# Softmax denominators of four token tiles in one 128-column block, and a new order of steps on four engines

## The reference

```python
x = x + tanh(g_xattn[0]) * xattn(layernorm(x), ctx, ctx, ...)
x = x + tanh(g_ffn[0]) * ffn(layernorm(x), w_gate, w_expert, b_expert)

# xattn: 16 heads of 32 features
scores = einsum('bhqd,bhkd->bhqk', Q, K) / sqrt(32)
out = einsum('bhqk,bhkd->bhqd', softmax(scores), V)
expert = (einsum('bsd,eod->ebso', out, We) + be).mean(axis=0)
return expert @ Wo.T + bo

# ffn: gate over 8 experts, the first 100 tokens that choose an expert are taken
best = argmax(softmax(hs @ w_gate)); locations = cumsum(one_hot(best)) - 1
combined = combine @ (dispatched @ w_expert + b_expert)
```

## Time and profile before

| | |
|---|---|
| time, median of 3 runs | 405.29 us (405.26 to 406.44) |
| the profiled execution | 405.64 us, span 403.9 us |
| granted TensorE clock | 1.000 in the whole span but its last microseconds |
| PE | busy 396.3 us (98%), 3102 matmuls |
| DVE | busy 333.3 us (83%) |
| ACT | busy 225.3 us (56%) |
| POOL | busy 167.4 us (41%) |

### The profile page before, as it was taken

One profiled execution on the slowest core, in us unless ns is written; L12 is line 12 of the kernel. 1 busy time (PEld: TensorE's weight loads), 2 busy tenths in 40 slices (PEclk: granted clock), 3 DMA queues, 4 the chain that ended last, 5 costly groups with the idle time before them and its releaser, 6 DMA issues.

```text
span 403.9 us, 8706 instructions
## 1 busy us (share of the span) xinstructions
PE 396.3 (98%) x3102; PEld 182.2 (45%) x3102; DVE 333.3 (83%) x662; ACT 225.3 (56%) x320; POOL 167.4 (41%) x157
## 2 busy tenths in 40 slices
PE   7999999999999999999999999999999999899996
PEld 4556454443444444444444434444444444354444
DVE  6548456986898989998998998899897589779996
ACT  4436323568566754947485486748556474775110
POOL 2028999215080247309033530713271064460371
PEclk9999999999999999999999999999999999999999
DMA  8999991466059408823960692295169016241585
GB/s 278 334 389 394 344 390 41 91 124 165 2 111 199 174 1 170 217 98 85 175 223 1 142 238 104 60 183 189 54 133 242 5 33 175 84 132 28 99 172 180
DMA packets 65901, 63.19 MB, mean 156 GB/s; under 512 B 42277, under 2 KB 45617, under 8 KB 65859
## 3 DMA queue, kind: packets, MB, share of 16 engines
q1 hardware_dynamic: 60747, 56.19, 50.9%
q0 software_dynamic: 1632, 3.49, 3.1%
q10 hardware_dynamic: 3480, 2.96, 2.2%
HBM read 29.59 MB, written 12.98 MB: 105 GB/s over the span
## 4 chain that ended last, share of the span: by engine, by line
PE 71%; DVE 2%; issue 1%; ACT 1%; POOL 1%; DVEq 0%; ACTq 0%; POOLq 0%
PE ps L840 71%; ACT probs L1234 1%; PE ps L1161 0%; DVE xb L1567 0%; POOL known L1929 0%; POOL rstd L1929 0%; DVE bn_raw L1573 0%; ACT xn_hi L1234 0%; DVE xn L1500 0%; DVE base_cnt L1653 0%; DVE place_hot L1723 0%; POOL veps L1927 0%; ACT part_x L1234 0%; DVE xb L1865 0%; DVE wqT_lo L1678 0%
## 5 line engine op out<-in xcount | busy, mean ns | idle before, releaser
L1234 ACT ACTIVATE probs<-ps 120x1024 f32<-120x1024 f32 x64 | 62.0, 1024 | 19.4 <-PE ps L840 19.4
L1602 DVE TENSOR_REDUCE neg_max<-ps 128x16 bf16<-128x1920 f32 x32 | 68.7, 2148 | 3.7 <-PE ps L840 3.7
L1989 POOL TENSOR_TENSOR attn_lo<-attn,attn_hi 128x512 f16<-128x512 f32 x28 | 31.8, 1158 | 91.0 <-ACT attn_hi L1234 91.0
L840 PE MATMUL ps<-xnT_hi,wqT_hi 128*128 128x512 f16 x128 | 48.6, 380 | 0.0
L840 PE MATMUL ps<-mixT_hi,attn_hi 128*128 128x512 f16 x128 | 48.5, 379 | 0.0
L840 PE MATMUL ps<-mixT_lo,attn_hi 128*128 128x512 f16 x128 | 48.5, 379 | 0.0
L840 PE MATMUL ps<-xnT_lo,wqT_hi 128*128 128x512 f16 x128 | 48.5, 379 | 0.0
L1997 POOL TENSOR_TENSOR xb<-xb,mix_bias 128x512 f32<-128x512 f32 x32 | 39.6, 1271 | 15.4 <-DVE cb_col L1544 15.4
L1234 ACT ACTIVATE q_hi<-ps,bias_cols 128x512 f16<-128x512 f32 x32 | 22.1, 692 | 31.4 <-PE ps L840 31.4
L840 PE MATMUL ps<-q_stack,k_stack 97*128 97x512 f16 x128 | 33.9, 381 | 1.2 <-ACT probs L1234 1.0
L840 PE MATMUL ps<-probs,den_sel 120*32 120x256 f32 x512 | 34.1, 384 | 0.0
(11 more groups left out here) (279 smaller groups left out, 792.7 us busy)
## 6 DMA issues: line engine op xcount, KB each, us to landing
xb<-in_x_dram SPq DMA_DIRECT2D x8, 1024.0 KB, 6.1
q_stack<-q_hi SPq DMA_DIRECT2D x48, 128.0 KB, 2.4
out_dram<-xb SPq DMA_DIRECT2D x6, 1024.0 KB, 7.4
raw<-in_L_xattn_We_dram SPq DMA_DIRECT2D x5, 1024.0 KB, 10.3
q_stack<-q_lo SPq DMA_DIRECT2D x32, 128.0 KB, 2.4
xb<-in_L_xattn_We_dram SPq DMA_DIRECT2D x3, 1024.0 KB, 10.3
k_stack<-k_scratch SPq DMA_DIRECT2D x8, 360.0 KB, 4.6
k_scratch<-k_hi ACTq DMA_DIRECT2D x16, 120.0 KB, 7.9
```

The lines of the kernel that those rows point to most:

```text
L840: return e.matmul(out_, a, b, start=start, stop=stop, **kw)
L1234: return e.activation(out_, in_, func, **kw)
L1602: e.tensor_reduce(maxed[:, :, :, g], quad[:, :, 0:NT * SK].rearrange("p j (t s) -> p t j s", t=NT), AX.X, ALU.max, negate=True).then_inc(s ...
L1989: e.tensor_tensor(attn_lo[:, g, :], attn[:, g, :], attn_hi[:, g, :], ALU.subtract).then_inc(s_alo, 1)
```

## The change

Three things change.

1. The denominators of all four token tiles stand in 128 columns. `weight_sums` makes four products of 128 columns for each row group where it made two of 256; the selection matrix is one row of `den_sel` of which a window is taken. `reciprocal`, `rden_high` and `rden_low` work on 128 columns where they had 256. `spread_rden` makes four products of 128 columns where it made two of 256. The setup builds `head_sel` with four DVE instructions of 512 columns instead of two.
2. The tables of PE, ACT, DVE and POOL are written in another order.
3. The first of the units that are done beside batch 0's queries (`N_FIRST`) waits for `route_x_out` of batch 0, since `route_x` now stands ahead of it by less.

The core of the diff:

```diff
-        den_sel = sb("den_sel", [SK, 2 * NK * DK + 24], F32)
-        head_sel = sb("head_sel", [P, 2, NK, P], F16)
+        den_sel = sb("den_sel", [SK, 2 * DK + NK], F32)
+        head_sel = sb("head_sel", [P, NT, NK, P], F16)
...
-        rden = sb("rden", [P, SH], F32)
+        rden = sb("rden", [P, SQ], F32)
...
+                if i == N_FIRST:
+                    e.wait_ge(s_pxe, 1)
...
-                for h in range(2):
-                    sel = den_sel[:, (h * NK + g) * DK:(h * NK + g + 1) * DK]
+                for t in range(NT):
+                    first = SEL_AT - (2 * t * NK + g)
                     for j in range(HJ):
                         row = slice(j * DK, (j + 1) * DK)
-                        ins = mm(den_b[row, 0:SH], sel, probs[:, g % 2, j, h * SH:(h + 1) * SH],
-                                 start=(g == 0 and h == 0), stop=(g == NK - 1 and h == 1))
+                        ins = mm(den_b[row, 0:SQ], den_sel[:, first:first + DK], probs[:, g % 2, j, t * SQ:(t + 1) * SQ],
+                                 start=(g == 0 and t == 0), stop=(g == NK - 1 and t == NT - 1))
...
-                mm(bank[:, 0:SH], head_sel[:, 0, g, :], rden_both[:, :])
-                mm(bank[:, SH:S], head_sel[:, 1, g, :], rden_both[:, :]).then_inc(s_bc, 1)
+                for t in range(NT):
+                    ins = mm(bank[:, t * SQ:(t + 1) * SQ], head_sel[:, t, g, :], rden_both[:, :])
+                ins.then_inc(s_bc, 1)
...
             run(range(0, B - 2), [
-                (logits, -1, 0), (table_rows, -2, 0), (scores, 0, 1), (values, 0, 0), (scores, 0, 2),
+                (logits, -1, 0), (table_rows, -2, 0), (scores, 0, 1), (values, 0, 0), (values, 0, 1),
+                (route_x, 1, 0), (scores, 0, 2), (q_begin, 1, 0), (q_end, 1, 0), (gate_mix, 0, 0), (scores, 0, 3),
...
-                e.reciprocal(rden[:, :], den_b[:, 0:SH]).then_inc(s_rec, 1)
+                e.reciprocal(rden[:, :], den_b[:, 0:SQ]).then_inc(s_rec, 1)
...
-            attn_lows = [(attn_low, 0, g) for g in range(NK)]
-            batch = [(rstd1, 2, 0), (rstd2, -1, 0)] + attn_lows + [(add_bias, 1, 0)]
-            run(range(-1, 2), batch)
-            clear_rows(0, 0)
-            run(range(2, B - 2), batch)
+            run(range(0, B - 2), [
+                (clear_rows, 0, 0), (rstd1, 2, 0), (rstd2, -1, 0), (add_bias, 1, 0), (attn_low, 0, 0),
+                (attn_low, 0, 1), (attn_low, 0, 2), (attn_low, 0, 3),
+            ])
```

More of the change, by code:

```diff
@@ L59 @@
 HALF = B // 2
-SH = S // 2
+SQ = S // NT
+SEL_AT = DK
 QK_SCALE = 16.0
@@ L1129, in _ @@
+                (max_scores, 1, 3), late_unit(2), (max_turn, 1, 0), late_unit(3), (scores, 1, 0), late_unit(4),
+                late_unit(5),
             ])
             run(range(0, B - 2), [
[L1132 to L1134 removed]
@@ L1142, in _ @@
+                (mix_low, 0, 1), (max_turn, 1, 0), (mix_middle, 0, 2), (mix_low, 0, 2), (mix_high, 0, 3),
+                (scores, 1, 0), (mix_low, 0, 3),
             ])
             run([B - 2], [
-                (logits, -1, 0), (table_rows, -2, 0), (scores, 0, 1), (values, 0, 0), (scores, 0, 2),
-                (values, 0, 1), (route_x, 1, 0), (scores, 0, 3), (q_begin, 1, 0),
-                (places, -1, 0), (q_end, 1, 0), (values, 0, 2), (max_scores, 1, 0), (values, 0, 3),
-                (q_tile, 1, 1), (q_begin, 1, 2), (spread_rden, 0, 0), (spread_rden, 0, 1), (q_end, 1, 2),
@@ L1150, in _ @@
-                (max_scores, 1, 1), (spread_rden, 0, 2), (spread_rden, 0, 3), (q_tile, 1, 3),
-                (mix_high, 0, 0), (max_scores, 1, 2), (mix_low, 0, 0), (mix_high, 0, 1),
-                (max_scores, 1, 3), (route_attn, 0, 0), (mix_low, 0, 1), (mix_begin, 0, 2), (max_turn, 1, 0),
-                (mix_middle, 0, 2), (logits, 0, 0), (mix_low, 0, 2), (mix_high, 0, 3), (scores, 1, 0),
-                (mix_low, 0, 3), (table_rows, -1, 0), (places, 0, 0),
+                (logits, -1, 0), (table_rows, -2, 0), (scores, 0, 1), (values, 0, 0), (values, 0, 1),
@@ new lines, in _ @@
+                (route_x, 1, 0), (scores, 0, 2), (q_begin, 1, 0), (q_end, 1, 0), (scores, 0, 3), (places, -1, 0),
+                (values, 0, 2), (values, 0, 3), (max_scores, 1, 0), (q_tile, 1, 1), (spread_rden, 0, 0),
+                (spread_rden, 0, 1), (q_begin, 1, 2), (spread_rden, 0, 2), (max_scores, 1, 1), (spread_rden, 0, 3),
+                (q_end, 1, 2), (q_tile, 1, 3), (max_scores, 1, 2), (mix_high, 0, 0), (mix_low, 0, 0),
+                (max_scores, 1, 3), (route_attn, 0, 0), (mix_high, 0, 1), (max_turn, 1, 0), (mix_low, 0, 1),
@@ L1156, in _ @@
+                (mix_begin, 0, 2), (logits, 0, 0), (mix_middle, 0, 2), (mix_low, 0, 2), (scores, 1, 0),
+                (mix_high, 0, 3), (places, 0, 0), (table_rows, -1, 0), (mix_low, 0, 3),
             ])
@@ new lines, in _ @@
+                (normalise1, 2, 0), (stats2, -1, 3), (moments2, -1, 0), (normalise1, 2, 1), (normalise1, 2, 2),
+                (logit_scale, -1, 0), (read_places, -1, 0), (x_lo, 2, 0), (gate_value, -1, 0), (reciprocal, 0, 0),
+                (gate_mix_low, 0, 0), (q_low, 1, 0), (rden_low, 0, 0), (maxima, 1, 0), (divide, 0, 0),
+                (q_low, 1, 1), (divide, 0, 1), (enter_rows, -1, 0), (x_lo, 2, 1), (divide, 0, 2), (divide, 0, 3),
+                (q_low, 1, 2), (maxima, 1, 1), (normalise1, 2, 3), (q_low, 1, 3), (maxima, 1, 2), (x1_tile, 0, 0),
@@ L1769, in _ @@
+                (maxima, 1, 3), (x_lo, 2, 2), (x1_tile, 0, 1), (enter_places, -1, 0), (x_lo, 2, 3),
+                (route_sum, 0, 0), (x1_tile, 0, 2), (part_low, 0, 0), (stats2, 0, 0), (stats2, 0, 1),
                 (x1_tile, 0, 3),
```

123 lines of the change are left out of this document (57 added, 66 removed).

## The result

The changed kernel takes **412.32 us** (median of 4 runs, 411.71 to 413.28), the kernel before 405.27: ratio 1.0172, interval 1.0154 to 1.0189. It is 7.0 us slower; 403.0 was predicted, 402.0 to 405.6.

The account below looks back on a forecast made before the run. PE, busy 98%, was taken to bound the kernel. Terms −0.9 − 0.25 + 0.2 + 0.1 − 0.3 − 0.3 − 1.2 + 0.4 = −2.25 took the profiled 405.64 to 403.39, or 403.0 as median; own range 402.2 to 404.0.

Parts of the forecast that it names:

- the new waits together I put at +0.4 (0 to 2): Thin slacks of the new POOL and DVE order, such as `attn_low` to `mix_low`: new waits cost +0.4 us in all.
- rival A: Thin slacks become waits where layer-norm tile meets `attn_low` and `x_lo` meets `add_bias`: 404.6 us, +4.8 at most; chance 0.22.
- My counter-argument, `q_low` at 0.74 beside POOL: DVE's `q_low` amid the three `attn_lo` takes 0.74 us without loss; taken as the rule for the rest.
- The sign that I set for A: Last `attn_low` at 1.6 us instead of 1.16, or a layer-norm tile of more than 0.5, would show rival A.
- Steady batch, −0.15: Middle batches: one block in column groups fewer saves 0.20 us, a wait for the values' bank costs 0.05, each batch.
- Denominators +0.3: Denominator passes of 128 columns cost +0.2 us, the spread of the reciprocals' 128-column products +0.1.
- Rival C: Passes of 128 columns no longer hide their weight loads, 27.5 ns per set of four: 409.8 us; chance 0.10.
- Batch 0, −0.3 and −0.15: Batch 0: the gate's wait for ACT's high part goes, −0.3 us; the steady batch's −0.20 + 0.05 applies too.
- Ahead of batch 0, −0.3: Ahead of batch 0: `sum_lo` wait −0.43 us, a shape change −0.10, stacked queries +0.25; range −0.5 to +0.9.
- for which I had 0.25: Batch 0's scores, now 0.5 us earlier, wait for stacked queries by DMA: +0.25 us, by the median landing plus tail.
- Batch 6 and the turn to 7, −0.25 and −1.2: Batch 6 loses three shape changes, −0.25 us; moving `expert_low` back starts batch 7's chain up to 1.2 earlier, −1.2.
- That `expert_low` has nothing urgent behind it: Turn to batch 7: `expert_high` becomes late, but nothing of PE's needs the experts until after the values.

Follow-up runs that it names:

- e3: Changed kernel with POOL's bias additions moved back behind the four `attn_low` in batches 0 to 5: 407.33 us.
- e2: Changed kernel's new order on all engines, but denominators, reciprocal and spread of 256 columns as before: 417.92 us.
- e5: Changed kernel with the last statistics and moments of the second norm ahead of DVE's first normalised tile in batches 0 to 5: 407.90 us.
- e15: Changed kernel with POOL's bias additions waiting until DVE has done the gate's small subtraction: 412.28 us.
- e7: Kernel before with POOL's bias additions ahead of the attention low parts from batch 1 on, and `clear_rows` ahead of batch 1: 427.40 us.
- e1: Kernel before, all tables in the old order, with only the new denominators of 128 columns: 406.02 us; two of 12 runs 410.1 and 411.4.
- e9: e3 with the old tables ahead of batch 0 on all four engines: 412.14 us.
- e11: e9 with gathers 1 to 7 held until the last denominators of batch 7: 406.87 us.
- e13: e11 with gathers 0 and 1 at once and only 2 to 7 held: 404.00 us, ratio 0.9968 to the kernel before.
- e12: e3 with gathers 1 to 7 held until the last denominators of batch 7: 408.11 us.
- e8: e3 with TensorE's idle warm-up products at the start cut in eight: 404.94 us; three of 12 runs 407.3 to 409.0.
- e4: Changed kernel with `gate_exp` behind `value_out` of group 2 on ACT in batches 0 to 5: 416.28 us.
- e6: Old order in batches 0 to 5; new order ahead of batch 0 and in batch 6, new denominators: 405.83 us.

## Why the prediction was wrong

**The step that failed is "the new waits together I put at +0.4 (0 to 2)".** They are 1.69 us a batch (37.51 against the 35.82 that PE needs by e3), 8.4 us in batches 1 to 5, and they have one source, a chain on DVE that has grown longer than PE's work. I looked at slacks of single steps and took the duration of every DVE instruction from the old trace, although I had noted as rival A that neither neighbour had been seen before. Rival A had the right mechanism and a wrong price: one tile of 0.45 beside `attn_low`, 404.6. It named `x_lo` beside `add_bias` without a price, and the two small instructions, the subtraction and the reciprocals' low part, not at all. The trace shows four instructions that lose 1.07 + 0.68 + 0.48 + 0.26 = 2.5 us a batch; and three of them are held up by `add_bias`, of which I said only that it fits into POOL's idle time. My counter-argument, `q_low` at 0.74 beside POOL, was true and proved nothing for the others: it reads one operand from PSUM. (The sign that I set for A, a tile of more than 0.5, was no sign: a tile by itself is recorded with 0.55; 0.47 is the spacing of four.)

Behind this stands a second omission: I never added up DVE's batch. At 83% busy I treated it as cover. The new order makes DVE wait 1.47 + 0.93 us for POOL; with that and the 2.5 its chain is 37.51 us long and PE's 35.82 is no longer the bound. With the lengths of each run's own trace the sum comes out in three kernels, and in the fourth it falls below PE's work, which then bounds:

| kernel | DVE's chain against the changed one | by the sum | batch |
|---|---|---|---|
| e2 | +0.80 −0.34 | 37.97 | 38.07 |
| e5 | −0.86 | 36.65 | 36.67 |
| e15 | −1.07 +0.27 | 36.71 | 36.72 |
| e3 | −2.2 | 35.3, below PE | 35.82 |

The exclusion itself is shown by e3, e7 and e15: each cures or makes just the lengths that lie beside POOL's instructions. The Trainium skill, "GPSIMD Engine Reference", section "Key points", states the contention for VectorE instructions with two SBUF inputs or in a 2-port mode, and "SBUF — State Buffer", section "SBUF: two separate sides", calls it an exclusive lock held for the whole instruction. The traces agree: 0.18 with one input and 0.93 with two, 0.2 us apart in e7, and a wait that lasts to the end of POOL's instruction whatever the columns; in the other direction, POOL's addition that begins beside `x_lo` lasts 1.71 for 1.26. For the layer-norm tile, which has one input, the trace shows the length (0.81, held to the end of the last `attn_low`) but not the mode; in e3, where it starts late in the third `attn_low`, the tile keeps 0.56 and the fourth takes 1.34 instead of 1.16. A rule that I quoted ahead of the result I should have priced for every such pair.

The other steps:
- **Steady batch, −0.15**: right; 35.82 in e3, −0.13, once DVE is out of the way.
- **Denominators +0.3**: 0.6 in e1. In the middle batches right (0.89 against 0.88 a group). What I left out is batch 7, where PE stops in some runs (0.4 us at the fourth denominators in e1's trace). Rival C is wrong: the loads are hidden.
- **Batch 0, −0.3 and −0.15**: right, −0.4 (36.44 to 36.02). It has no gate of an earlier batch, so the chain above is not in it.
- **Ahead of batch 0, −0.3**: wrong, +0.5 (the first denominators come at 91.5 to 92.8 in the traces with the new start, at 91.0 to 91.4 in those with the old one). The wait at 80.72 went, but the maxima, moved behind `sum_low`, are late in their turn:

```profile
70.61 0.39 PE L841 MATMUL ps<-k_hi,q_hi 32*128 32x120 f16 x16 [0.37 <-DVE neg_max L1589]
...
80.09 0.39 PE L841 MATMUL ps<-k_hi,q_hi 32*128 32x120 f16 x16 [0.44 <-DVE neg_max L1589]
...
86.41 1.02 PE L841 MATMUL ps<-q_stack,k_stack 97*128 97x512 f16 x4 [0.44 <-DMA q_stack<-shift]
```

  Here too the exclusion acts. POOL makes its bias additions at 74.39, where the kernel before makes them at 89.11, and the two quarters of `sum_low` ahead of the third maxima, with two inputs in SBUF, take 2.44 us where two took 1.28. At 86.41 the scores wait 0.44 for their stacked queries, for which I had 0.25:

```profile
75.44 2.44 DVE L1523 SCALAR_TENSOR_TENSOR sum_lo<-w_sum,sum_hi 128x512 f16<-128x512 f32 x2
77.80 2.15 DVE L1589 TENSOR_REDUCE neg_max<-ps 128x16 bf16<-128x1920 f32 x1
...
74.39 5.84 POOL L1975 TENSOR_TENSOR xb<-xb,mix_bias 128x512 f32<-128x512 f32 x4
```

- **Batch 6 and the turn to 7, −0.25 and −1.2**: −1.1 together. The subtraction came 1.19 us behind the second denominators of batch 7 (348.88 and 347.69), now 0.50 (355.36 and 354.86), so the chain is 0.7 us earlier, not 1.2; of the two waits of 0.69 and 0.31 the first went and the second stayed, since ACT needs its 1 us for each half in any order.
- **That `expert_low` has nothing urgent behind it**, and that spread, POOL's total and the slack of `attn_low` hold, was not contradicted.

What stays open: why PE stops in batch 7 beside the gathers. Shown is that holding the gathers takes the stops of e9 away (e11, e13); for e3's the hold of e12 does it, but so did other warm-up products in e8. All traces with stops have short passes; the kernel before has none in its trace, and its runs lie between 404.5 and 407.0 but for a single one of 2290.8. Gathers beside short passes are not enough, though: the first gather starts 2.6 us ahead of the third denominators of batch 7 in e3, e4, e9 and e15, which stop, and just so in the changed kernel, e5 and e6, which do not. Nor are the stops only between short products: e3's longest, 1.16 us, stands ahead of a full one. Whether it is the supply of instructions, which come by DMA, is only argued. Of the unequal times of e4 and e15 against their batches, 2.6 us each are these stops in the traces; the rest is not shown.

## What to carry to other kernels

When steps are moved, the durations of the old trace hold only for the neighbours of the old trace: list the VectorE instructions with two SBUF operands that come to lie beside GpSimd's large ones and price each, however small, at up to one whole GpSimd instruction. And add up the batch of every engine above 80% in its new order, its waits included, since the longest chain sets the period and single slacks say nothing about it. A wait that a profile shows on the bounding engine may be only where another engine's lateness comes out (e4): moving the step behind it wins nothing.

## What the runs showed of the hardware

- An 8-column VectorE addition with two SBUF inputs takes up to 1.19 us beside GpSimd's additions of 1.26 us, 0.19 alone; one order of GpSimd's steps costs 22 us (e7), of which PE's waits for such additions are 13.5.
- It holds in the other direction: GpSimd's addition of 1.26 us takes 1.71 where a VectorE instruction of 512 columns with two SBUF inputs got in first (changed kernel, batch 3).
- After an idle time of 2.2 us TensorE's products of 512 columns started 0.43 apart instead of 0.216, until 361.8: its lower clock level, 1.2 of 2.4 GHz. The windows of e11, the last columns granted clock, DMA share and GB/s:

```profile
350.00:355.50 5.50, 5.50 (x88) 2.83 (x80) 3.46 (x8) 3.51 (x6) 1.80 (x2) 1.00 0.08 21
358.00:362.00 4.00, 3.98 (x19) 2.27 (x20) 1.60 (x4) 1.99 (x4) 3.09 (x4) 0.57 0.53 150
```

- Short fp32 products (128 columns, four side by side) run at the rate of longer ones in the middle batches (0.89 us a group, 0.88 with 256 columns). Beside eight row gathers PE stopped for 0.3 to 1.0 us each among them in e9 and not in the changed kernel; the cause is open.
